# The queries of chunks 1 to 3 as three fp32r products of high and low parts

## The chip, the cores and the metric

The kernel runs on one core of one Trainium2 chip. The metric is the device time of one execution in microseconds. The core has five engines that run side by side and meet only in semaphores: TensorE (PE, with its weight loads PEld), VectorE (DVE), ScalarE (ACT), GpSimd (POOL), and SyncE (SP), which issues most transfers. Matrix products land in PSUM, which has eight banks of 128 partitions x 512 fp32 numbers.

## The reference, cut to what matters

Three blocks one behind the other, each on a layer norm of its input and added to it: cross attention of 64 items (32 queries of 256 channels, 257 context rows of 192 channels, 16 heads), an attention over the items, and a mixture of eight experts. The change touches one line of the first block, the projection of the queries.

```python
q = (query @ Wq + bq).reshape(B, Nq, H, D).transpose(0, 2, 1, 3)   # B 64, Nq 32, Cq 256, H 16, D 16
k = (key_value @ Wk + bk) ...                                        # Nkv 257, Ckv 192
v = (key_value @ Wv + bv) ...
attn = jnp.einsum('bhqd,bhkd->bhqk', q, k) * scale                   # then clip and softmax
x = jnp.einsum('bhqk,bhkd->bqhd', attn, v).reshape(B, Nq, Cq)
return x @ Wo + bo
```

## The kernel before

The cross attention runs over 64 tiles, i = 0 to 63, one item each. It is a software pipeline: in iteration i TensorE (loop at line 1127) does `scores(i)`, `weigh(i-2)`, the two `transp(i-1)`, then `kproj(i+1)` in two halves and `vproj(i+1)`. DVE (loop at 882) does `clip(i,0)`, `negmax(i,0)`, `clip(i,1)`, `ptevac(i-1)`, `negmax(i,1)`, then `total`, `recip` and `otevac` of older tiles. ACT (loop at 969) does the other `ptevac`, the four exponentials, and the copies of keys and values out of PSUM. POOL (loop at 761) splits the context into high and low parts, spreads the queries for the heads (`spread`), and does the small products `tailpart` and `norm`.

The queries are made for 512 rows at a time, a chunk of 16 tiles: chunk 0 before the loop, chunks 1 to 3 in iterations 11/12, 27/28 and 43/44. In iteration 16c-5 TensorE transposes the normalised input (`qturn`, 1015, two banks "t") and ACT copies both banks to `xnT` (`qchunk`, 912), which gives `s_t0e`. In iteration 16c-4, behind `vproj`, TensorE makes the products with the fp32 weights `Wq` (`qproj`, 1024, two banks "q"), and DVE adds the bias and scales at the end of its own iteration (`qevac`, 812).

Keys and values are already made of fp32r products: each operand is copied to fp32r (the high part), the difference to the fp32 original is the low part, and high x high, high x low and low x high are summed in PSUM (`terms`, 1033). Weights of the later stages are split in the same way in quiet iterations: ACT makes the high part (994), POOL the low part (`wlow`, 691).

PSUM banks 4 to 7 go round in a fixed order, the list `uses` (226 to 239). Each entry is a key, and the semaphore with its value that tells that the bank's content has been read. `take` (1008) gives the n-th use bank 4 + n % 4 and first waits until use n-4 is released. In iteration 11 the list has p(10,0), p(10,1), k(12,0), k(12,1), v(12), t(1,0), t(1,1), and in iteration 12 p(11,0), p(11,1), k(13,0), k(13,1), v(13), q(1,0), q(1,1). Every engine works through its own instructions in order, and the order above is written out by hand.

Of the kernel before, what the change touches and what calls it, by code (L numbers as in the profile page):

```python
# [6 lines left out]
ALU = mybir.AluOpType  # L7
# [24 lines left out]
C_MN = 168  # L32
# [43 lines left out]
def build(nc, d, out, vx_d, w1_d, y_d, g_d):  # L76
    ctx = ExitStack()
    with ctx:
# [56 lines left out]
        s_c = sem("s_c")  # L135
        s_w = sem("s_w")
        s_w3 = sem("s_w3")
        s_c2 = sem("s_c2")
        s_id = sem("s_id")
        s_v2 = sem("s_v2")  # L140
        s_fill = sem("s_fill")
# [74 lines left out]
        Mb = put("Mb", [128, 2, 4, 16])  # L216
        rc = put("rc", [128, 2, 4])
        nm = put("nm", [128, 2, 4])
        wst.append(put("wst1", [128, 1024]))
        whl.append(put("whl1", [128, 2, 1024], F32R))  # L220

# [5 lines left out]
        for i in range(-1, T + 1):  # L227
            if 1 <= i:
                uses += [(("p", i - 1, p), s_pte[p], i) for p in range(2)]
            if i + 1 < T:  # L230
                uses += [(("k", i + 1, p), s_ke, 2 * (i + 1) + p + 1) for p in range(2)]
            if i + 1 < T:
                uses += [(("v", i + 1), s_ve, i + 2)]
            if i == 0:
                uses += [(("b",), s_basee, 1)]
            if 0 <= i < 48 and i % 16 == 11:
                uses += [(("t", i // 16 + 1, k), s_t0e, 2 * (i // 16 + 1) + k + 1) for k in range(2)]
            if 0 <= i < 48 and i % 16 == 12:
                uses += [(("q", i // 16 + 1, m), s_qe, 2 * (i // 16 + 1) + m + 1) for m in range(2)]
        spot = {u[0]: n for n, u in enumerate(uses)}  # L240
# [3 lines left out]

        def whalves(n):

            if n == 0:
                return [WaR[:, w, :, :].rearrange("p k n -> p (k n)") for w in range(2)]
            return [WcR[:, w, n - 1, :] for w in range(2)]
# [312 lines left out]
        with nc.Block() as block:  # L562

            @block.sync
            def _(sp):
# [26 lines left out]
                load_ctx(1)  # L592
                sp.dma_start(Wo[:, :, :], d["xWo"].rearrange("(k p) n -> p k n", p=128)).then_inc(s_w3, 16)
                sp.dma_start(bcc[:, :, :], bcast(d["brow"], 128)).then_inc(s_w3, 16)
                sp.dma_start(cst[:, C_MN:C_END], d["cst"][:, C_MN:C_END]).then_inc(s_c2, 16)
                load_ctx(2)
                sp.wait_ge(s_vxe, 2)
                sp.wait_ge(s_v1, 2)
# [37 lines left out]
                for j in range(3, NPAIR):  # L636
                    load_ctx(j)
                    for q in range(2 * E):
                        if j == 6 + 3 * q // 2:
                            for h in range(2):  # L640
                                pace(j, h)
                                load_piece(q, h)
                    for q in range(2 * E):
                        if j == 8 + 3 * q // 2:
                            for n in range(4):
                                pace(j, 2 + n)
                                store_split(q, n // 2, n % 2)
                    if j in (5, 12, 20):
                        c = (5, 12, 20).index(j) + 1
                        load_tails(16 * c, 16, s_vt[c])  # L650
                    if j in (7, 15):
                        load_x((7, 15).index(j) + 2)
                    if j == 3:

                        sp.wait_ge(s_wl, 1)
                        sp.dma_start(wA[:, 0, :].rearrange("p (k n) -> p k n", k=2),
                                     d["aW"].rearrange("(k p) n -> p k n", p=128)).then_inc(s_w2, 16)
                        sp.dma_start(wA[:, 1, :], d["cwT"][0:128].rearrange("p k n -> p (k n)")).then_inc(s_w2, 16)
                        sp.dma_start(WgT[:, :, :], d["WgT"].rearrange("(k p) n -> p k n", p=128)).then_inc(s_w2, 16)
                    if j == 10:  # L660
                        sp.wait_ge(s_wsd, 4)
                        sp.dma_start(wA[:, 0, :], d["cwT"][128:256].rearrange("p k n -> p (k n)")).then_inc(s_ws, 16)
                    if j == 25:

                        sp.wait_ge(s_t0, 8)
                        for n in range(8):
                            pace(j, 2 + n)
                            t0 = 4 * (n // 2)
                            sp.dma_start(xb[64 * (n % 2):64 * (n % 2) + 64, t0:t0 + 4, :], xbd[n % 2][:, t0:t0 + 4, :]
                                         ).then_inc(s_xb, 16)  # L670

            @block.gpsimd
            def _(g):
# [16 lines left out]

                def wlow(n, h):

                    g.wait_ge(s_wsh, n + 1)
                    hi, lo = whalves(n)
                    c = slice(256 * h, 256 * h + 256)
                    g.tensor_tensor(lo[:, c], wA[:, n % 2, c], hi[:, c].bitcast(F32), ALU.subtract).then_inc(s_wsd, 1)
                    g.wait_ge(s_wsd, 2 * n + h + 1)

                rstd(0)

# [60 lines left out]
                for i in range(T + 2):  # L761
                    if i + 1 < T:
                        spread(i + 1)
                    if 1 <= i <= T:
                        tailpart(i - 1)

                    j, n = (i + 3) // 2 if i % 2 else (i + 2) // 2, 0 if i % 2 else 2
                    go = 2 <= j < NPAIR
                    if go:
                        split(j, n)  # L770
                    if i >= 2:
                        norm(i - 2)
                    if go:
                        if n == 2:
                            g.wait_ge(s_m, i - 1)
                        split(j, n + 1)

                    q = (i - 9) // 3
                    if i % 3 == 0 and 0 <= q < 2 * E:
                        g.wait_ge(w_h, q + 1)  # L780
                        g.tensor_tensor(whl[q % 2][:, 1, :], wst[q % 2][:, :], whl[q % 2][:, 0, :].bitcast(F32),
                                        ALU.subtract).then_inc(w_l, 1)

                    if i % 16 == 6 and i < 48:
                        rstd(i // 16 + 1)
                    if i in (10, 12, 14, 16, 30, 32):
                        m = (10, 12, 14, 16, 30, 32).index(i)
                        wlow(m // 2, m % 2)
                    if i == 49:
                        g.wait_ge(s_xb, 128)  # L790
                        g.wait_ge(s_basee, 1)
                    if 49 <= i < 49 + NTILE:
                        m = i - 49
                        g.tensor_tensor(xb[:, m, :], xb[:, m, :], base[:, :], ALU.add).then_inc(s_xbb, 1)
                        g.wait_ge(s_xbb, m + 1)

            @block.vector
            def _(v):
# [37 lines left out]

                def base_row():

                    v.wait_ge(s_c2, 16)
                    v.wait_ge(s_base, 1)  # L840
                    v.tensor_tensor(base[:, :], held("b")[:, 0:C], bcc[:, 0, :], ALU.add).then_inc(s_basee, 1)

                def clip(i, p):
                    v.wait_ge(s_s, 2 * i + p + 1)
# [37 lines left out]
                for i in range(T + 3):  # L882
                    if i < T:
                        clip(i, 0)
                        negmax(i, 0)
                        clip(i, 1)
                        if i >= 1:
                            ptevac(i - 1)
                        negmax(i, 1)
                    if 2 <= i < T + 2:  # L890
                        total(i - 2)
# [19 lines left out]
            def _(a):  # L911
                def qchunk(c):
                    for k in range(2):
                        a.wait_ge(s_t0, 2 * c + k + 1)
                        if c:
                            a.wait_ge(s_q, 2 * c)
                        a.activation(xnT[:, k, :], held("t", c, k)[:, :], ACT.Copy).then_inc(s_t0e, 1)

                def highs(j):
                    a.wait_ge(s_cx[j], 48)  # L920
# [48 lines left out]
                for i in range(-1, T + 1):  # L969
# [16 lines left out]
                    if i % 3 == 2 and 0 <= q < 2 * E:  # L986
                        a.wait_ge(w_d[q % 2], 32 * (q // 2 + 1))
                        if q >= 2:
                            a.wait_ge(w_s[q % 2], 64 * (q // 2))
                        a.activation(whl[q % 2][:, 0, :], wst[q % 2][:, :], ACT.Copy).then_inc(w_h, 1)  # L990
                    if i in (9, 11, 29):
                        n = (9, 11, 29).index(i)
                        a.wait_ge([s_w2, s_w2, s_ws][n], [48, 48, 16][n])
# [3 lines left out]
            def _(t):  # L997
# [25 lines left out]

                def qproj(c):
                    t.wait_ge(s_t0e, 2 * c + 2)
                    for m in range(2):
                        b = take("q", c, m)
                        for k in range(2):
                            mm = t.matmul(b[:, :], Wq[:, k, 128 * m:128 * m + 128], xnT[:, k, :],
                                          start=(k == 0), stop=(k == 1))  # L1030
                        mm.then_inc(s_q, 1)

                def terms(b, bi):
# [81 lines left out]

                def base_row():

                    t.wait_ge(s_c2, 16)
                    t.wait_ge(s_w3, 16 * 2)
                    b = take("b")  # L1120
                    for k in range(2):
                        mm = t.matmul(b[:, 0:C], bcol[:, 4 + k:5 + k].broadcast_to([128, 128]), Wo[:, k, :],
# [87 lines left out]
            def _(t):  # L1210
                t.wait_ge(s_ote, T)
                t.wait_ge(s_w2, 48)
                t.wait_ge(s_wsd, 6)

                def take(*key):
                    n = place[key]
# [807 lines left out]
```

## Time and profile before

| | |
|---|---|
| median of 3 runs | 610.33 us (609.41 to 612.26) |
| the profiled execution | 609.9 us, span 608.1 us |
| TensorE busy | 588.9 us, 97% |
| DVE busy | 457.2 us, 75% |
| ACT busy | 337.2 us, 55% |
| POOL busy | 321.3 us, 53% |
| mean granted TensorE clock | 0.994 |

The profile is of one execution; times in it count from the span's start. An engine's busy time is the union of its instructions. A row of the timeline is "start, length, engine, line, operation, output <- inputs", with the idle time before it and who ended it in square brackets. Matmuls are pipelined: their rows overlap, so the distance from start to start is what one costs. The attention loop runs from about 15 to 334 us.

### The profile page before, as it was taken

Reading aid. Unit: us, or ns where it says so; the run is one execution under the profiler, and the core shown is the slowest. Engines: PE = TensorE matmul, PEld = TensorE weight load, DVE = VectorE, ACT = ScalarE, POOL = GpSimd, SP = SyncE. Lnnn points to the kernel's source line nnn. Section 1 sums busy time; section 2 is a strip of 40 time slices with the busy share of each in tenths; the row PEclk is TensorE's granted clock in tenths of the full one; section 3 lists DMA queues with packets and bytes.
Section 4 is the critical chain, followed back from the end, with each engine's and each line's share of the span. In section 5 each row is a group of like instructions: output and inputs, shape, how many; then the busy total and the mean of one; then the engine's idle time right before and its main releaser. Section 6 shows DMA issues by size and latency. Waiting matters only on the chain.

```text
span 608.1 us, 21788 instructions
## 1 busy us (share of the span) xinstructions
PE 588.9 (97%) x8367; PEld 482.3 (79%) x8367; DVE 457.2 (75%) x1069; ACT 337.2 (55%) x751; POOL 321.3 (53%) x474
## 2 busy tenths in 40 slices
PE   9999999999999999999999999998899999998977
PEld 4888878888788887888887788884588888884865
DVE  4688877888678886777777676888788888883654
ACT  3677868878687786777776156454323333330211
POOL 3457858787578777678874311111433333314771
PEclk9999999999999999999999999998999999999899
DMA  8724653776354855875400797257333334434884
GB/s 226 182 74 110 172 180 99 246 183 212 110 193 127 246 157 175 199 230 153 150 16 3 307 416 285 67 178 253 128 131 130 131 130 133 131 124 131 232 251 118
DMA packets 66069, 102.11 MB, mean 168 GB/s; under 512 B 15504, under 2 KB 42192, under 8 KB 65072
## 3 DMA queue, kind: packets, MB, share of 16 engines
q1 hardware_dynamic: 60672, 86.42, 44.2%
q0 software_dynamic: 4432, 13.50, 8.1%
q8 instruction: 69, 1.13, 0.8%
q10 hardware_dynamic: 864, 0.79, 0.5%
q14 instruction: 32, 0.26, 0.1%
HBM read 69.42 MB, written 31.26 MB: 166 GB/s over the span
## 4 chain that ended last, share of the span: by engine, by line
PE 54%; POOL 23%; issue 14%; DVE 3%; DMA 2%; ACT 2%; POOLq 0%; DVEq 0%; ACTq 0%
PE bank L1936 12%; PE scores L1936 6%; PE bank L1044 5%; PE bank L1051 5%; PE bank L1076 4%; POOL hA L718 4%; POOL lA L714 4%; POOL cg L1768 4%; POOL hA L710 4%; PE scores L1092 3%; PE scores L1065 3%; POOL Mb L751 2%; POOL tm L742 2%; PE bank L1961 1%; PE scores L1921 1%
## 5 line engine op out<-in xcount | busy, mean ns | idle before, releaser
L850 DVE TENSOR_SCALAR Pm<-scores 128x514 f32<-128x514 f32 x128 | 88.0, 688 | 52.8 <-PE scores L1065 52.6
L966 ACT ACTIVATE Pm<-Pm,nm 128x257 f32<-128x257 f32 x256 | 115.8, 505 | 2.5 <-DVE nm L855 2.5
L855 DVE TENSOR_REDUCE nm<-Pm 128x2 f32<-128x514 f32 x128 | 87.4, 683 | 2.2
L1757 POOL DMA_INDIRECT Xg<-y_d,inv x39 | 37.0, 950 | 82.9 <-PE scores L1921 70.1
L961 ACT ACTIVATE PT<-bank 128x512 f32<-128x512 f32 x64 | 38.3, 598 | 74.0 <-PE bank L1076 74.0
L1044 PE MATMUL bank<-hA,wH 128*128 128x258 f32 x256 | 75.2, 304 | 0.3 <-POOL hA L718 0.3
L1076 PE MATMUL bank<-cst,Pm 128*128 128x128 f32 x512 | 70.0, 279 | 0.0
L1044 PE MATMUL bank<-hA,wL 128*128 128x258 f32 x256 | 69.3, 281 | 0.0
L1051 PE MATMUL bank<-wH,hA 128*128 128x256 f32 x256 | 69.0, 281 | 0.0
L1051 PE MATMUL bank<-wL,hA 128*128 128x256 f32 x256 | 68.9, 280 | 0.0
L1895 ACT ACTIVATE sg<-sg 128x512 f32<-128x512 f32 x39 | 24.7, 632 | 77.6 <-DVE sg L1782 77.6
L1936 PE MATMUL bank<-W,xh 128*128 x208 | 66.7, 402 | 0.5 <-DVE xl L1849 0.5
L1092 PEld LDWEIGHTS scores<-Vs,PT 128*32 128x32 f32 x4096 | 41.2, 110 | 25.2 <-issue 24.1
L751 POOL TENSOR_TENSOR Mb<-Os,rc 128x64 f32<-128x64 f32 x64 | 21.6, 338 | 73.6 <-DVE rc L875 73.2
L1076 PEld LDWEIGHTS bank<-cst,Pm 128*128 128x128 f32 x512 | 54.9, 141 | 2.9 <-issue 0.8
L944 ACT ACTIVATE kT<-bank,bcol 128x258 f32<-128x258 f32 x128 | 53.5, 469 | 2.6 <-PE bank L1044 2.3
L1044 PEld LDWEIGHTS bank<-hA,wH 128*128 128x128 f32 x256 | 48.4, 189 | 1.2 <-issue 1.1
L1044 PEld LDWEIGHTS bank<-hA,wL 128*128 128x128 f32 x256 | 48.5, 189 | 0.2 <-issue 0.2
L1051 PEld LDWEIGHTS bank<-wL,hA 128*128 128x128 f32 x256 | 48.2, 188 | 0.0
L1051 PEld LDWEIGHTS bank<-wH,hA 128*128 128x128 f32 x256 | 48.2, 188 | 0.0
L1092 PE MATMUL scores<-Vs,PT 128*32 128x17 f32 x4096 | 47.5, 186 | 0.2 <-issue 0.2
L1768 POOL DMA_INDIRECT cg<-g_d,pi x32 | 31.7, 992 | 26.5 <-DMA g_d<-gg 17.0
(280 smaller groups left out, 1434.1 us busy)
## 6 DMA issues: line engine op xcount, KB each, us to landing
w_d<-whl SPq DMA_DIRECT2D x64, 256.0 KB, 3.5
W<-w_d SPq DMA_DIRECT2D x6, 2048.0 KB, 16.7
g_d<-gg SPq DMA_DIRECT2D x39, 256.0 KB, 2.4
wst<-in_W1T SPq DMA_DIRECT2D x32, 256.0 KB, 3.3
cx<-in_ctxT SPq DMA_DIRECT2D x31, 258.0 KB, 3.0
cx<-in_ctxT SPq DMA_DIRECT2D x62, 129.0 KB, 3.5
bb<-in_b SPq DMA_DIRECT2D x8, 512.0 KB, 6.3
W<-w_d SPq DMA_DIRECT2D x5, 512.0 KB, 5.3
```

Source lines behind the costliest of these rows:

```text
L850: v.tensor_scalar(Pm[:, i % 2, 2 * p:2 * p + 2, :], S4[:, 2 * p:2 * p + 2, 0:NK], -CLAMP, CLAMP, ALU.max, ALU.min).then_inc(s_cl, 1)
L855: v.tensor_reduce(nm[:, i % 2, 2 * p:2 * p + 2], Pm[:, i % 2, 2 * p:2 * p + 2, :], AX.X, ALU.max, negate=True).then_inc(s_nm, 1)
L944: a.activation(kT[:, i % 2, m, :], held("k", i, m)[:, 0:NKP], ACT.Identity, bias=bcol[:, 2 + m:3 + m]).then_inc(s_ke, 1)
L961: a.activation(PT[:, i % 2, 0, :, :].rearrange("p a b -> p (a b)"), held("p", i, 0)[:, :], ACT.Copy).then_inc(s_pte[0], 1)
L966: a.activation(Pm[:, i % 2, g, :], Pm[:, i % 2, g, :], ACT.Exp, bias=nm[:, i % 2, g:g + 1]).then_inc(s_ex, 1)
L1044: mm = t.matmul(b[:, 0:NKP], w[:, 128 * m:128 * m + 128], c, start=(e == 0), stop=(e == 4))
L1051: mm = t.matmul(b[:, C * c:C * c + C], x[:, 128 * c:128 * c + 128], w[:, C:2 * C], start=(e == 0), stop=(e == 4))
L1076: mm = t.transpose(b[:, o:o + 128], Pm[:, i % 2, 2 * p + gg, 128 * c:128 * c + 128], ident)
L1092: mm = t.matmul(pO[r, VH * g:VH * g + VH], PT[:, i % 2, p, 2 * gg + c, r], Vs[:, i % 4, c, 4 * (h // 2) + g, h % 2, :], start=first, stop= ...
L1757: g.indirect_dma_start(out=Xg[:, i % 3, :], out_offset=None, in_=y_d, in_offset=bass.IndirectOffsetOnAxis(ap=inv[:, i:i + 1], axis=0)).the ...
L1768: g.indirect_dma_start(out=cg[:, j % 8, k, :], out_offset=None, in_=g_d, in_offset=bass.IndirectOffsetOnAxis(ap=pi[:, k, j:j + 1], axis=0) ...
L1936: mm = t.matmul(o, x[:, i % 2, k, :], W1[:, bass.DynSlice(w + (part * 2048 + k * 1024 + 512 * h), 512)], start=(k == 0 and part == 0 and x ...
```

## The change

Chunk 0 stays as it is. For chunks 1 to 3 ACT copies the transposed input to fp32r (`xqR[:, 0]`), DVE subtracts that from the bank for the low part (`xqR[:, 1]`, the new function `query_lows`, placed in iteration 16c-4 between `ptevac` and the second `negmax`), and `qproj` sums three fp32r products for each half of the channels where it had plain fp32 ones. The release of the "t" banks in `uses` becomes `s_xl`, given by `query_lows`. `Wq` is split too: the high part by ACT at i=4, the low part by POOL at i=5 and i=7. The counts of `s_wsh` and `s_wsd` shift by one and two for that. The semaphore `s_c2` is merged into `s_w3`. Two new arrays, `WqR` (4 KB of a partition) and `xqR` (8 KB), are put ahead of `wst1` and `whl1`.

```diff
@@ -135,7 +135,7 @@
         s_c = sem("s_c")
         s_w = sem("s_w")
         s_w3 = sem("s_w3")
-        s_c2 = sem("s_c2")
+        s_xl = sem("s_xl")
         s_id = sem("s_id")
         s_v2 = sem("s_v2")
         s_fill = sem("s_fill")
@@ -216,6 +216,8 @@
         Mb = put("Mb", [128, 2, 4, 16])
         rc = put("rc", [128, 2, 4])
         nm = put("nm", [128, 2, 4])
+        WqR = put("WqR", [128, 2, 2, C], F32R)
+        xqR = put("xqR", [128, 2, 2, 512], F32R)
         wst.append(put("wst1", [128, 1024]))
         whl.append(put("whl1", [128, 2, 1024], F32R))
 
@@ -234,7 +236,7 @@
             if i == 0:
                 uses += [(("b",), s_basee, 1)]
             if 0 <= i < 48 and i % 16 == 11:
-                uses += [(("t", i // 16 + 1, k), s_t0e, 2 * (i // 16 + 1) + k + 1) for k in range(2)]
+                uses += [(("t", i // 16 + 1, k), s_xl, 2 * (i // 16) + k + 1) for k in range(2)]
             if 0 <= i < 48 and i % 16 == 12:
                 uses += [(("q", i // 16 + 1, m), s_qe, 2 * (i // 16 + 1) + m + 1) for m in range(2)]
         spot = {u[0]: n for n, u in enumerate(uses)}
@@ -244,6 +246,8 @@
 
         def whalves(n):
 
+            if n == -1:
+                return [WqR[:, w, :, :].rearrange("p k n -> p (k n)") for w in range(2)]
             if n == 0:
                 return [WaR[:, w, :, :].rearrange("p k n -> p (k n)") for w in range(2)]
             return [WcR[:, w, n - 1, :] for w in range(2)]
@@ -592,7 +596,7 @@
                 load_ctx(1)
                 sp.dma_start(Wo[:, :, :], d["xWo"].rearrange("(k p) n -> p k n", p=128)).then_inc(s_w3, 16)
                 sp.dma_start(bcc[:, :, :], bcast(d["brow"], 128)).then_inc(s_w3, 16)
-                sp.dma_start(cst[:, C_MN:C_END], d["cst"][:, C_MN:C_END]).then_inc(s_c2, 16)
+                sp.dma_start(cst[:, C_MN:C_END], d["cst"][:, C_MN:C_END]).then_inc(s_w3, 16)
                 load_ctx(2)
                 sp.wait_ge(s_vxe, 2)
                 sp.wait_ge(s_v1, 2)
@@ -658,7 +662,7 @@
                         sp.dma_start(wA[:, 1, :], d["cwT"][0:128].rearrange("p k n -> p (k n)")).then_inc(s_w2, 16)
                         sp.dma_start(WgT[:, :, :], d["WgT"].rearrange("(k p) n -> p k n", p=128)).then_inc(s_w2, 16)
                     if j == 10:
-                        sp.wait_ge(s_wsd, 4)
+                        sp.wait_ge(s_wsd, 6)
                         sp.dma_start(wA[:, 0, :], d["cwT"][128:256].rearrange("p k n -> p (k n)")).then_inc(s_ws, 16)
                     if j == 25:
 
@@ -690,11 +694,12 @@
 
                 def wlow(n, h):
 
-                    g.wait_ge(s_wsh, n + 1)
+                    g.wait_ge(s_wsh, n + 2)
                     hi, lo = whalves(n)
                     c = slice(256 * h, 256 * h + 256)
-                    g.tensor_tensor(lo[:, c], wA[:, n % 2, c], hi[:, c].bitcast(F32), ALU.subtract).then_inc(s_wsd, 1)
-                    g.wait_ge(s_wsd, 2 * n + h + 1)
+                    whole = Wq[:, :, :].rearrange("p k n -> p (k n)") if n < 0 else wA[:, n % 2, :]
+                    g.tensor_tensor(lo[:, c], whole[:, c], hi[:, c].bitcast(F32), ALU.subtract).then_inc(s_wsd, 1)
+                    g.wait_ge(s_wsd, 2 * n + h + 3)
 
                 rstd(0)
 
@@ -783,9 +788,9 @@
 
                     if i % 16 == 6 and i < 48:
                         rstd(i // 16 + 1)
-                    if i in (10, 12, 14, 16, 30, 32):
-                        m = (10, 12, 14, 16, 30, 32).index(i)
-                        wlow(m // 2, m % 2)
+                    if i in (5, 7, 10, 12, 14, 16, 30, 32):
+                        m = (5, 7, 10, 12, 14, 16, 30, 32).index(i)
+                        wlow(m // 2 - 1, m % 2)
                     if i == 49:
                         g.wait_ge(s_xb, 128)
                         g.wait_ge(s_basee, 1)
@@ -836,9 +841,18 @@
 
                 def base_row():
 
-                    v.wait_ge(s_c2, 16)
+                    v.wait_ge(s_w3, 48)
                     v.wait_ge(s_base, 1)
                     v.tensor_tensor(base[:, :], held("b")[:, 0:C], bcc[:, 0, :], ALU.add).then_inc(s_basee, 1)
+
+                def query_lows(c):
+
+                    for k in range(2):
+                        v.wait_ge(s_t0e, 2 * c + k + 1)
+                        if c >= 2:
+                            v.wait_ge(s_q, 2 * c)
+                        v.tensor_tensor(xqR[:, 1, k, :], held("t", c, k)[:, :], xqR[:, 0, k, :].bitcast(F32), ALU.subtract
+                                        ).then_inc(s_xl, 1)
 
                 def clip(i, p):
                     v.wait_ge(s_s, 2 * i + p + 1)
@@ -886,6 +900,8 @@
                         clip(i, 1)
                         if i >= 1:
                             ptevac(i - 1)
+                        if i < 49 and i % 16 == 12:
+                            query_lows(i // 16 + 1)
                         negmax(i, 1)
                     if 2 <= i < T + 2:
                         total(i - 2)
@@ -912,9 +928,10 @@
                 def qchunk(c):
                     for k in range(2):
                         a.wait_ge(s_t0, 2 * c + k + 1)
-                        if c:
+                        if c >= 2:
                             a.wait_ge(s_q, 2 * c)
-                        a.activation(xnT[:, k, :], held("t", c, k)[:, :], ACT.Copy).then_inc(s_t0e, 1)
+                        a.activation(xqR[:, 0, k, :] if c else xnT[:, k, :], held("t", c, k)[:, :], ACT.Copy
+                                     ).then_inc(s_t0e, 1)
 
                 def highs(j):
                     a.wait_ge(s_cx[j], 48)
@@ -988,6 +1005,8 @@
                         if q >= 2:
                             a.wait_ge(w_s[q % 2], 64 * (q // 2))
                         a.activation(whl[q % 2][:, 0, :], wst[q % 2][:, :], ACT.Copy).then_inc(w_h, 1)
+                    if i == 4:
+                        a.activation(whalves(-1)[0], Wq[:, :, :].rearrange("p k n -> p (k n)"), ACT.Copy).then_inc(s_wsh, 1)
                     if i in (9, 11, 29):
                         n = (9, 11, 29).index(i)
                         a.wait_ge([s_w2, s_w2, s_ws][n], [48, 48, 16][n])
@@ -1023,11 +1042,21 @@
 
                 def qproj(c):
                     t.wait_ge(s_t0e, 2 * c + 2)
+                    if c:
+                        t.wait_ge(s_xl, 2 * c)
+                        t.wait_ge(s_wsd, 2)
                     for m in range(2):
                         b = take("q", c, m)
-                        for k in range(2):
-                            mm = t.matmul(b[:, :], Wq[:, k, 128 * m:128 * m + 128], xnT[:, k, :],
-                                          start=(k == 0), stop=(k == 1))
+                        s = slice(128 * m, 128 * m + 128)
+                        if c == 0:
+                            for k in range(2):
+                                mm = t.matmul(b[:, :], Wq[:, k, s], xnT[:, k, :], start=(k == 0), stop=(k == 1))
+                        else:
+                            e = 0
+                            for k in range(2):
+                                for w, x in ((0, 0), (1, 0), (0, 1)):
+                                    mm = t.matmul(b[:, :], WqR[:, w, k, s], xqR[:, x, k, :], start=(e == 0), stop=(e == 5))
+                                    e += 1
                         mm.then_inc(s_q, 1)
 
                 def terms(b, bi):
@@ -1115,8 +1144,7 @@
 
                 def base_row():
 
-                    t.wait_ge(s_c2, 16)
-                    t.wait_ge(s_w3, 16 * 2)
+                    t.wait_ge(s_w3, 48)
                     b = take("b")
                     for k in range(2):
                         mm = t.matmul(b[:, 0:C], bcol[:, 4 + k:5 + k].broadcast_to([128, 128]), Wo[:, k, :],
@@ -1210,7 +1238,7 @@
             def _(t):
                 t.wait_ge(s_ote, T)
                 t.wait_ge(s_w2, 48)
-                t.wait_ge(s_wsd, 6)
+                t.wait_ge(s_wsd, 8)
 
                 def take(*key):
                     n = place[key]
```

## Rows read from the trace of the kernel before

**Rows 1.** The page, part 1: busy us, share of span, instructions.

```profile
PE 588.9 (97%) x8367; PEld 482.3 (79%) x8367; DVE 457.2 (75%) x1069; ACT 337.2 (55%) x751; POOL 321.3 (53%) x474
```

**Rows 2.** Windows: busy us of each engine in a stretch, clock, DMA share, GB/s.

```profile
102.00:150.00 48.00, 48.00 (x1156) 42.43 (x1149) 40.66 (x94) 38.01 (x85) 38.99 (x57) 1.00 0.68 200
```

**Rows 3.** The chain of work, 69 to 90 us: start, us, what.

```profile
74.55 0.62 PE scores L1065 x16
...
76.86 1.21 PE bank L1044 x10
...
79.26 3.43 PE bank L1029 x8
82.69 0.62 PE scores L1065 x16
...
87.38 0.62 PE scores L1065 x16
```

**Rows 4.** Timeline of TensorE, scores and first key weights, tile 12's iteration.

```profile
74.47 0.69 PE L1065 MATMUL scores<-kT,QF 32*64 32x258 f32 x16
...
76.59 0.19 PEld L1044 LDWEIGHTS bank<-hA,wH 128*128 128x128 f32 x1
```

**Rows 5.** Timeline of DVE, tile 12's iteration.

```profile
77.14 0.68 DVE L862 COPY PT<-bank 128x512 f32<-128x512 f32 x1
77.74 0.68 DVE L855 TENSOR_REDUCE nm<-Pm 128x2 f32<-128x514 f32 x1
...
81.01 0.75 DVE L816 TENSOR_SCALAR qT<-bank,bcol 128x512 f32<-128x512 f32 x1 [2.06 <-PE bank L1029]
```

**Rows 6.** Timeline of ACT, the copies out of the "t" banks.

```profile
74.20 1.08 ACT L917 ACTIVATE xnT<-bank 128x512 f32<-128x512 f32 x2
```

**Rows 7.** Cover on ACT and POOL: groups, waits and timeline, 22 to 79 us.

```profile
L961 ACT ACTIVATE PT<-bank 128x512 f32<-128x512 f32 x4 | 2.4, 600 | 5.1 <-PE bank L1076 5.1
...
L696 POOL TENSOR_TENSOR WaR<-wA,WaR x2: 732/734/735, 71.0 to 82.9; 128x256 fp32r<-128x256 f32 x2
...
POOL Mb L751 <- DVE rc L875: 12.6, 8, 1.9
...
78.84 0.29 POOL L751 TENSOR_TENSOR Mb<-Os,rc 128x64 f32<-128x64 f32 x1 [2.97 <-DVE rc L875]
```

**Rows 8.** Timeline of TensorE and DVE, tile 44's iteration (chunk 3).

```profile
234.00 0.69 PE L1065 MATMUL scores<-kT,QF 32*64 32x258 f32 x16
...
237.26 0.68 DVE L855 TENSOR_REDUCE nm<-Pm 128x2 f32<-128x514 f32 x1
```

**Rows 9.** Like forms elsewhere: the chain at 437 us, DVE's low parts (ns).

```profile
437.30 2.77 PE bank L1936 x12
...
446.27 2.74 PE bank L1936 x12
...
L1444 DVE TENSOR_TENSOR xTl<-scores,xTh x5: 659/681/692, 353.7 to 388.3; 128x512 fp32r<-128x512 f32 x5
```

**Rows 10.** Timeline: hand-overs from DVE to a waiting TensorE.

```profile
433.46 0.42 DVE L1849 TENSOR_TENSOR xl<-scores,xh 128x256 fp32r<-128x256 f32 x1
434.04 0.31 PEld L1936 LDWEIGHTS bank<-W,xh 128*128 128x128 f32 x2 [0.76 <-issue]
...
561.97 0.75 DVE L1871 SCALAR_TENSOR_TENSOR zc<-cg,cmb,zc 128x512 f32<-128x512 f32 x1
562.77 0.29 PEld L1947 LDWEIGHTS scores<-cst,zc 128*128 128x128 f32 x2 [2.30 <-DVE zc L1871]
```

**Rows 11.** Two gaps of TensorE and the windows behind them (clock third from last).

```profile
562.77 1.12 PE L1947 MATMUL scores<-cst,zc 128*128 128x128 f32 x4 [2.06 <-DVE zc L1871]
...
562.90:566.00 3.10, 3.10 (x10) 2.65 (x11) 1.24 (x2) 0.60 (x1) 2.49 (x3) 0.50 0.72 202
...
592.97 0.66 PE L1947 MATMUL scores<-cst,zc 128*128 128x128 f32 x4 [1.71 <-DVE zc L1871]
...
593.00:596.30 3.30, 3.30 (x20) 2.97 (x21) 2.19 (x5) 1.07 (x2) 1.68 (x2) 1.00 0.81 210
```

## The prediction

> **What bounds the kernel now.** I read the page's first part first. TensorE is busy for 588.9 of 608.1 us (97%) [rows 1], so a microsecond put into its queue, or a microsecond for which it must wait, is likely to be a microsecond of the time. That is an average, so the stage that the change touches comes next: the windows of the attention loop [rows 2]. From 102 to 150 us TensorE is busy for all 48.00 us at clock 1.00, while DVE, ACT and POOL have 7 to 10 us of room each. The chain of work over one chunk border [rows 3] gives the beat: the scores of tiles 12, 13 and 14 stand in it at 74.55, 82.69 and 87.38. An ordinary tile takes 82.69 to 87.38 = 4.69 us; tile 12 takes 8.14, with the 3.43 us of qproj in it. In this stretch the chain names TensorE alone. So the loop runs at TensorE's pace, and what the change does has to be read as: how many microseconds fewer in qproj, and does TensorE begin to wait for somebody.
>
> **The change, part by part.**
>
> *qproj of chunks 1 to 3.* Removed: four fp32 products of 512 columns, which the trace shows as 8 records that take 3.43 us of the chain [rows 3]. Added: twelve fp32r products of 512 columns with 128x128 weights. The same set is in the trace: an expert step of line 1936 is twelve such products and takes 2.74 to 2.77 us of the chain [rows 9], say 2.75 or 0.229 each. That is 0.68 us less per chunk. The Trainium skill (TensorE: Matmul & The Clock Gate, section "Back-to-back issue gap") gives about 131 ns for one 512-column product in a sustained stream of loads and products. By that figure the twelve would be 1.57 us and the saving 1.86 per chunk, an estimate from the page; this trace's 0.229 for the same pair of instructions speaks against it.
>
> *The bank of the transposed queries.* This is where I expect the cost. The four PSUM banks go round in the order of `uses`. After the two "t" banks of chunk c come p(11,0), p(11,1), then k(13,0), k(13,1): so kproj of tile 13, first half, waits in `take` for the release of ("t", c, 0), and the second half for ("t", c, 1). Before, the release was s_t0e, given by ACT's two copies from 74.20 to 75.28 [rows 6], over a microsecond before TensorE asked at 76.59 [rows 4]. Now the release is s_xl, which DVE gives after query_lows, and DVE runs query_lows in iteration 12 behind clip(12,0), negmax, clip(12,1) and the copy of p(11,1). In the trace DVE starts that copy at 77.14 and its next instruction at 77.74 [rows 5]. In the new order that next instruction is the low part of k=0. Its form (128x512 fp32r from PSUM and SBUF) is in the trace on line 1444: 0.68 us [rows 9]. So the bank is free at 77.74 + 0.68 = 78.42. The hand-over from DVE to TensorE's weight load is 0.05 us in one row (DVE ends at 561.97 + 0.75 = 562.72, load at 562.77) and 0.16 in another (433.46 + 0.42 = 433.88, load at 434.04) [rows 10]. The first weight load of kproj then starts at 78.47 to 78.58 in place of 76.59: a wait of 1.88 to 1.99 us, new, on the engine that bounds. I take 1.90, as most of DVE's path to it is plain and the 0.16 row has a register read beside it. Queued behind this wait are kproj, vproj, qproj and the scores of tile 13; all of it moves back as one.
>
> The second low part ends 0.60 later (DVE's starts lie 0.60 apart [rows 5]), at 79.02. The first half of kproj takes 1.20 / 2 = 0.60 us [rows 3], so the second half asks at about 79.1: no second wait. qproj itself waits for s_xl as well, long past then. The other chunks look alike: in the third the scores start at 234.00 and DVE's slot for the low part is at 237.26 [rows 8], 3.26 us later, as 77.74 is 3.27 after 74.47, the start of the scores of tile 12 [rows 4]; the second has the same pattern. So three times the same.
>
> *Work that only moves DVE, ACT and POOL.* DVE gets 2 x 0.60 = 1.20 us in iteration 12, ahead of negmax(12,1). That makes exp of heads 2 and 3 of tile 12 later. They now wait for negmax to end at about 79.6 and for the two kevac copies behind the delayed kproj, so they run from about 80.4 to 81.3. The transposes that need them come after the scores of tile 13, at 83.9 or later: covered by over 2 us. DVE waited 2.06 us for qproj [rows 5], which takes up its 1.20. The query evacuation keeps its place right behind the last product, so clip(13,0) follows it as before. The copy of the high part on ACT has the size of the copy that it replaces. One more ACT copy of 512 columns at i=4 costs 0.60 us (the copy of 128x512 in [rows 7]) against an idle 5.1 / 4 = 1.28 us before each transposed-P copy; two more POOL subtractions of 0.73 at i=5 and i=7 go against a POOL that waits 12.6 / 8 = 1.6 us for recip in an iteration there [rows 7]. All at nothing. If their cover were gone, they would cost 0.60 and 1.46 us once. DVE's s_xl waits stand behind ACT's copies that ended long before. POOL's norm(10), which waits for recip, comes 1.2 us later; POOL had waited 2.97 us there [rows 7], and its next product for TensorE, the query spread of tile 14, is due 4.7 us after tile 13's scores: covered. The merged semaphores (s_c2 into s_w3) wait for the same three transfers. SP's own order is unchanged; its paced transfers go with the tiles.
>
> *The sum.* Per chunk +1.90 - 0.68 = +1.22 us, three chunks +3.7 us (bounds 3 x 1.20 to 3 x 1.31: 3.6 to 3.9). The profiled execution took 609.9 us (span 608.1), 0.4 under the median of the runs. 609.9 + 3.7 = 613.6, and on the median 610.33 + 3.7 = 614.0. Everything behind the loop starts from its last tile, so I let the shift through one for one.
>
> **The rivals.**
>
> *A. TensorE's clock falls after the new gap.* A gap of some 1.9 us in front of a dense stream is new in this loop. The combine stage at the end has two such gaps: after 2.06 us idle the clock is 0.50 (1.2 GHz of 2.4) for at least 3.1 us, after 1.71 us idle it stays at 1.00 [rows 11]. The new gap lies between them. The loop before it is dense, which speaks against a fall; its length speaks for one. A fall costs about half of 3.1 us or a little more, 1.6 us, since TensorE bounds: one fall gives 615.6, three give 618.8. The Trainium skill (TensorE: Matmul & The Clock Gate, "What's actually happening") puts it as "the default state is throttled, and activity releases the throttle"; by that rule thin activity should throttle it again, and the fall after 2.06 us agrees.
>
> *B. The wait does not bite: no slower, a little faster.* If DVE gave the "t" banks back before TensorE asks for them, at 76.59, only the saving stays: 3 x 0.68 = 2.0 us, 608.3 us. The point is a wait of 0.68 us per chunk: below it the change wins. For it: DVE has some 7 us of room in 48 [rows 2], so it is not short of time as such. Against it: its idle time in these iterations lies before the scores and before qproj's end, and the code puts the low parts behind three instructions that start only with them; DVE's slot would have to come 1.2 us sooner.
>
> *C. Part of the loss is given back.* TensorE's pause lets POOL, ACT and the transfers get ahead, and where TensorE waits a little for them later, that wait goes. With TensorE busy for all of a 48 us stretch [rows 2] there is little to win: 0.3 to 1 us, 613.0 to 613.7, or down to 611.8 if the low part is handed over more quickly than its row.
>
> *D. The change does not do what it says*: the products run as more than twelve passes, or at fp32's rate (12 x 0.86 = 10.3 us in place of 3.43, +20 us in all). The fp32r rows of the same size say no.
>
> **How the numbers follow.** Forecast, wait of 1.9 and clock kept: 0.50, own range 613.2 to 615.2. A: 0.26, 615.6 to 618.8. C: 0.15, 611.8 to 613.7. B: 0.08, 608 to 610.5. D: 0.01. The predicted time is 614.0. The range for 8 in 10 leaves out B and the cases with two or three falls: 611.3 to 617.5. Half a per cent, 3.05 us, is about what a measurement of this kernel can tell from no change, so "slower" begins at 613.4, close under my forecast. Slower: 0.42 from the forecast, 0.25 from A and 0.02 from C and D, 0.69. Same: the rest of the forecast, nearly all of C and half of B, 0.26. Faster: 0.05.
>
> **What would show it.** In the profile after: 24 fp32 records at line 1029's successor are gone and 36 fp32r ones stand there, about 2.75 us per chunk; TensorE idle for about 1.9 us before the first kproj product of tiles 13, 29 and 45, released by DVE's xqR; tile 12, 28 and 44 take about 9.4 us from scores to scores in place of 8.14; DVE's wait for qproj shrinks to under 2 us. All other tiles keep 4.69. The clock at the three places shows A. If the kproj products start at once, the bank argument is wrong; if the gap is there and the total is not, the loss came back behind the loop and one-for-one is wrong.

## The result

The changed kernel takes 615.64 us (median of 8 runs, 612.74 to 617.10) against 610.95 us of the kernel before (8 runs, 608.21 to 612.26): ratio 1.0077 with a 95% interval of 1.0051 to 1.0102. It is slower by 3.1 to 6.2 us. 614.0 was forecast.

The page of the changed kernel, part 1 and, from part 5, the group of key products that now waits (against [rows 1]). The columns of a group are: line, engine, operation, output<-inputs, shape, count, busy us, mean ns, idle before and who ended it.

```profile
span 614.6 us, 21828 instructions
...
PE 589.0 (96%) x8379; PEld 482.8 (79%) x8379; DVE 460.8 (75%) x1075; ACT 338.8 (55%) x752; POOL 323.6 (53%) x476
...
L1073 PE MATMUL bank<-hA,wH 128*128 128x258 f32 x256 | 75.3, 305 | 5.1 <-DVE xqR L854 4.9
```

TensorE is not busier (589.0 us against 588.9), the span is longer, and 4.9 us of idle time in front of kproj, absent before, end with DVE's low part (line 854). The 2 us that the cheaper products save hardly show in the busy time: in the loop it is 312.1 us in place of 313.0, behind the loop 264.5 in place of 263.4. The chain over the first chunk border (start, length, what), to be read against [rows 3]:

```profile
74.55 0.64 PE scores L1094 x16
...
76.54 0.68 DVE Pm L864
77.22 0.10 DVE PT L876
77.32 0.42 issue
77.74 0.69 DVE xqR L854
78.43 0.04 issue
78.48 1.46 PE bank L1073 x10
79.93 1.18 PE bank L1080 x10
81.11 2.76 PE bank L1058 x12
83.87 0.62 PE scores L1094 x16
...
88.56 0.62 PE scores L1094 x16
```

From scores to scores the step over the border is 83.87 - 74.55 = 9.32 us, against 8.14 before. qproj takes 2.76 in place of 3.43. But the chain now leaves TensorE: from the scores it runs through DVE's clip, copy and low part, and comes back to kproj only at 78.48. Only 1.62 us of the wait are idle time of TensorE's products; the rest is a first key piece of 1.46 in place of 1.21 [rows 3]. The next step is the ordinary 4.69 again. DVE, ACT and TensorE in the same stretch, from the timeline (against [rows 4 to 6]):

```profile
75.21 0.69 DVE L864 TENSOR_SCALAR Pm<-scores 128x514 f32<-128x514 f32 x1 [2.02 <-PE scores L1094]
77.74 1.28 DVE L854 TENSOR_TENSOR xqR<-bank,xqR 128x512 fp32r<-128x512 f32 x2
82.54 0.75 DVE L821 TENSOR_SCALAR qT<-bank,bcol 128x512 f32<-128x512 f32 x1 [2.40 <-PE bank L1058]
...
74.20 1.08 ACT L933 ACTIVATE xqR<-bank 128x512 fp32r<-128x512 f32 x2
80.34 0.90 ACT L983 ACTIVATE Pm<-Pm,nm 128x257 f32<-128x257 f32 x2
...
78.47 0.19 PEld L1073 LDWEIGHTS bank<-hA,wH 128*128 128x128 f32 x1 [1.86 <-DVE xqR L854]
```

ACT has emptied both "t" banks by 75.28. DVE is idle for 2.02 us up to 75.21. It reads the same banks only at 77.74. TensorE's first weight load of kproj starts at 78.47, where it started at 76.59 before.

Read over the whole loop, by the start of each tile's scores (a step is named by the tile it leads into): the steps into tiles 13, 29 and 45 were 8.15, 8.13 and 8.15 us and are 9.32, 9.32 and 9.34, together 3.55 us more. The last tile's scores start 5.87 us later (333.81 against 327.94). The other 2.3 us are what is left of three longer steps of this execution, 2.8 us together, and some slightly shorter ones: 5.12 into tile 20 (4.69 before), 6.31 into tile 28 (5.57) and 6.29 into tile 55 (4.69). From the last tile's scores to the end it takes 280.8 us in place of 280.1. In the step into tile 55, TensorE stops in the middle of vproj and no engine is named as the releaser:

```profile
295.11 0.38 PE L1080 MATMUL bank<-wH,lA 128*128 128x256 f32 x1 [1.34 <-issue]
```

Whether such steps belong to the change was an open question, and one run below is for it.

### The profile page after: what moved, and what is told of

It is laid out like the page before. It is cut to its first block, busy times and chain, and to the rows that moved or that the text cites. A ratio compares the mean times of both kernels' runs of the same rounds, so it can differ in the third digit from the quotient of the medians.

```text
span 614.6 us, 21828 instructions
## 1 busy us (share of the span) xinstructions
PE 589.0 (96%) x8379; PEld 482.8 (79%) x8379; DVE 460.8 (75%) x1075; ACT 338.8 (55%) x752; POOL 323.6 (53%) x476
## 4 chain that ended last, share of the span: by engine, by line
PE 51%; POOL 22%; issue 15%; DVE 8%; DMA 2%; ACT 1%; POOLq 0%; DVEq 0%; ACTq 0%
PE bank L1964 12%; PE scores L1964 6%; PE bank L1073 6%; PE bank L1080 5%; PE bank L1105 4%; POOL cg L1796 4%; POOL hA L723 4%; POOL lA L719 4%; POOL hA L715 3%; PE scores L1121 3%; PE scores L1094 3%; POOL Mb L756 2%; POOL tm L747 2%; PE scores L1949 1%; PE bank L1989 1%
```

## The experiments

The first four ran on one chip beside the kernel before at 610.82 us (29 runs). The last four ran on another, where the kernel before takes 628.91 us (7 runs). The kernel before was timed there, but no trace of it is kept from that chip. The changed kernel's loop has ordinary steps of the same length on both; the time behind it is longer (298.6 us from the last tile's scores to the end in run 5, against 280.8). Ratios are always to the kernel before on the same chip.

**1. The low parts moved into DVE's idle time.**

```diff
                     if i < T:
+                        if i < 49 and i % 16 == 12:
+                            query_lows(i // 16 + 1)
                         clip(i, 0)
...
                             ptevac(i - 1)
-                        if i < 49 and i % 16 == 12:
-                            query_lows(i // 16 + 1)
                         negmax(i, 1)
```

> The changed kernel with one move: DVE makes the two low parts at the head of iteration 12 (28, 44), ahead of clip(i,0), in the time in which it waited 2.02 us for the scores, and no longer behind ptevac. Theory (the new cost is only the wait for the t banks): the banks come back at about 76.1, before TensorE asks at 76.59, no gap; scores to scores over the three borders 7.5 us in place of 9.32 (and 8.15 before the change); in all 3 x 0.68 = 2.0 us under the kernel before, about 608.5 to 609, 5.5 us under the changed kernel. Rival (the DVE work itself or the delayed clip costs): borders stay above 8.15, no gain on before. Rival (something behind the loop costs): borders 7.5 but the total no better than before.

Measured: 608.94 us (12 runs), ratio 0.9975 (0.9954 to 0.9996). All three steps over the borders are 7.45 us. Its chain over the first border:

```profile
75.25 0.62 PE scores L1094 x16
75.87 0.67 PE scores L1121 x51
76.54 1.02 PE bank L1105 x8
77.56 1.18 PE bank L1073 x10
78.75 1.18 PE bank L1080 x10
79.93 2.77 PE bank L1058 x12
82.70 0.62 PE scores L1094 x16
```

TensorE alone is in it, from scores to scores 7.45 us. In the timeline of DVE and ACT one sees what the move costs and that it is covered:

```profile
75.53 1.29 DVE L854 TENSOR_TENSOR xqR<-bank,xqR 128x512 fp32r<-128x512 f32 x2 [1.62 <-ACT xqR L933]
76.74 0.68 DVE L864 TENSOR_SCALAR Pm<-scores 128x514 f32<-128x514 f32 x1
...
78.18 0.91 ACT L983 ACTIVATE Pm<-Pm,nm 128x257 f32<-128x257 f32 x2 [0.24 <-DVE nm L869]
```

clip starts 0.8 us later behind the scores than in the changed kernel (76.74 - 75.18 against 75.21 - 74.48, the scores starting in the timeline at 75.18 and 74.48), ACT waits 0.24 us for the maxima, and nothing of it comes to TensorE. The DVE work is the same, only its place differs, so the loss was in the place. This version beats both kernels: 3 x (8.14 - 7.45) = 2.1 us in the steps, 0.2 to 2.8 us in the times.

**2. The same DVE work, but the banks released by ACT.**

```diff
-                uses += [(("t", i // 16 + 1, k), s_xl, 2 * (i // 16) + k + 1) for k in range(2)]
+                uses += [(("t", i // 16 + 1, k), s_t0e, 2 * (i // 16 + 1) + k + 1) for k in range(2)]
...
-                        v.tensor_tensor(xqR[:, 1, k, :], held("t", c, k)[:, :], xqR[:, 0, k, :].bitcast(F32), ALU.subtract
+                        v.tensor_tensor(xqR[:, 1, k, :], xqR[:, 0, k, :].bitcast(F32), xqR[:, 0, k, :].bitcast(F32), ALU.subtract
```

> The changed kernel with DVE's low-part instructions in their place and of the same size, but reading the high part from SBUF and not the t bank, which ACT's copy releases as before the change. Left out: the low part of the queries comes out as zero, so two of the six terms with it add nothing. Theory: same DVE, ACT, POOL and TensorE work, no wait at kproj, borders 8.15 - 0.68 = 7.47 us, total 2.0 us under before. Rival (DVE's 1.2 us in the middle of the iteration delays TensorE by itself, through exp and transposes): borders above 8.15.

Measured: 609.91 us (10 runs), ratio 0.9974 (0.9951 to 0.9998). The steps are 7.58, 8.11 and 7.57 us. kproj no longer waits at any border, with DVE's low parts still behind its copy of P. So the wait is that for the bank, and the delay of DVE's second maximum by 1.2 us is not what costs. The steps are above 7.47 because now qproj reaches the low parts early. In the second border it waits for them outright, since DVE's two subtractions took 1.81 us there and 1.28 at the others:

```profile
157.84 1.81 DVE L854 TENSOR_TENSOR xqR<-xqR 128x512 fp32r<-128x512 f32 x2
...
159.74 3.00 PE L1058 MATMUL bank<-xqR,WqR 128*128 128x512 f32 x12 [0.43 <-issue]
```

DVE ends at 159.65, qproj starts at 159.74. In the changed kernel this second wait is hidden behind the first.

**3. The wait with the old products.**

```diff
-                        if c == 0:
+                        if True:
                             for k in range(2):
-                                mm = t.matmul(b[:, :], Wq[:, k, s], xnT[:, k, :], start=(k == 0), stop=(k == 1))
+                                x = xqR[:, 0, k, :].bitcast(F32) if c else xnT[:, k, :]
+                                mm = t.matmul(b[:, :], Wq[:, k, s], x, start=(k == 0), stop=(k == 1))
```

> The changed kernel with its low parts and bank waits, but with the four fp32 products of before in qproj of chunks 1 to 3, reading the high part. Left out: the low part of the queries is computed and not used. Theory: the wait costs 1.86 us per border and the products take 3.43 again: borders 8.15 + 1.86 = 10.0 us, three times, total 5.6 us over before (about 616.5). Rival (part of the saving in the changed kernel came from elsewhere): borders other than 9.32 + 0.68 = 10.0.

Measured: 616.87 us (4 runs), ratio 1.0108 (1.0077 to 1.0140). The steps are 10.00, 10.01 and 10.01 us, 1.86 to 1.88 above the kernel before. Its chain:

```profile
77.81 0.69 DVE xqR L854
78.50 0.04 issue
78.54 1.47 PE bank L1074 x10
80.01 1.18 PE bank L1081 x10
81.19 3.43 PE bank L1054 x8
84.62 0.62 PE scores L1095 x16
```

The two terms are independent: the wait is 1.87 by itself, the products give back 0.68, and 8.14 + 1.87 - 0.68 = 9.33 is what the changed kernel shows.

**4. The splitting of the weights alone.** To the kernel before are added the copy on ACT and the two subtractions on POOL, with their counts:

```diff
+                    if i == 4:
+                        a.activation(whalves(-1)[0], Wq[:, :, :].rearrange("p k n -> p (k n)"), ACT.Copy).then_inc(s_wsh, 1)
...
-                    if i in (10, 12, 14, 16, 30, 32):
-                        m = (10, 12, 14, 16, 30, 32).index(i)
-                        wlow(m // 2, m % 2)
+                    if i in (5, 7, 10, 12, 14, 16, 30, 32):
+                        m = (5, 7, 10, 12, 14, 16, 30, 32).index(i)
+                        wlow(m // 2 - 1, m % 2)
```

> The kernel before with only the splitting of the query weights added: one ACT copy at i=4, two POOL subtractions at i=5 and i=7, results not used. Theory: hidden, tiles 4 to 9 keep 4.67 to 4.70 us, total as before within the noise. Rival (ACT or POOL work late somewhere, or the extra code shifts things): some tile between 4 and 9 longer by 0.3 us or more; or single longer tiles far from the change, as tiles 20, 28 and 55 of the changed kernel had (+0.43, +0.73, +1.6).

Measured: 609.67 us (10 runs), ratio 0.9990 (0.9963 to 1.0017). Each step into tiles 4 to 12 lies within 0.15 us of its length before, the steps over the borders are 8.14, 8.14 and 8.13. Hidden, as costed. The only step that is over 0.3 us longer than before, 5.31 into tile 3 (4.73), comes ahead of the added work; run 5 returns to it.

**5. The changed kernel once more**, unaltered, for the three long steps.

> The changed kernel unaltered, once more. The profiled execution of it was 6.5 us longer in span than the one of before, of which the three borders are 3.54 us; tiles 20, 28 and 55 were longer by 0.43, 0.73 and 1.6 us with no engine named as releaser. Theory (these three are chance, of the kind that both kernels have in single executions): borders 9.32 to 9.34 again, the long tiles elsewhere or absent, span near 611.6 plus or minus 1.5; median 3.5 to 4.5 us over before. Rival (the change brings them, as by the moved code or transfers): tile 55 is long by over 1 us again and the loop is about 5.9 us longer than before.

Measured: 632.17 us (5 runs), ratio 1.0049 (1.0030 to 1.0068), 3.1 us with 1.9 to 4.3 as its bounds. The steps over the borders are 9.34, 9.34 and 9.33 us. The steps into tiles 20 and 55 are ordinary here (4.78 and 4.69), that into 28 is 5.55 as before the change. So the three long steps do not come in every execution of the changed kernel. But this execution has a longer one, 8.56 us into tile 3 (4.73 before). TensorE stops there shortly before the end of `weigh`, again with no engine named, and its clock is 0.50 behind the stop:

```profile
30.18 0.29 PE L1121 MATMUL scores<-Vs,PT 128*32 128x17 f32 x2 [2.25 <-issue]
...
30.40:32.40 2.00, 2.00 (x12) 2.00 (x11) 0.69 (x1) 0.85 (x2) 0.00 (x0) 0.50 0.07 21
```

With it the last tile's scores start at 335.84, 7.9 us later than before the change, of which the borders are 3.6 and this step 3.8.

Such stops are not spread at random: they come back in front of the same product, with another length each time. The one into tile 3 stands in the traces of runs 1, 2, 4, 5, 6 and 7 (0.39 to 2.25 us), the one in vproj on the way into tile 55 in that of the result and in runs 1, 6, 7 and 8 (0.24 to 1.34 us). The first is in run 4 without the new products or the new wait. The second is in none of the traces of the kernel before and of runs 2 to 5, so from one trace or two of a kernel it can't be told whether the change makes it more likely. Others have their own places (6.06 into tile 52 in the next run). What makes them was not found.

**6. The low parts one instruction earlier**, ahead of the copy of P and behind the second clip.

```diff
+                        if i < 49 and i % 16 == 12:
+                            query_lows(i // 16 + 1)
                         if i >= 1:
                             ptevac(i - 1)
-                        if i < 49 and i % 16 == 12:
-                            query_lows(i // 16 + 1)
                         negmax(i, 1)
```

> The changed kernel with the low parts one instruction earlier: ahead of ptevac(i-1), behind clip(i,1). DVE's slots lie 0.60 us apart. Theory: the gap before kproj is 1.86 - 0.60 = 1.26 us, borders 9.32 - 0.60 = 8.72 us, total about 1.8 us under the changed kernel. Rival: the banks of the transposed P are copied 1.2 us later and something that needs them waits; then borders above 8.72.

Measured (one execution): steps of 8.70, 8.71 and 8.71 us, 0.62 under the changed kernel.

```profile
79.60 0.39 PE L1073 MATMUL bank<-hA,wH 128*128 128x258 f32 x1 [1.02 <-DVE xqR L854]
```

DVE's place sets the wait, one for one. The single time, 633.32 us, says nothing against it: it is one run, and its steps into tiles 3, 52 and 55 are 6.39, 6.06 and 5.60 us long.

**7. and 8. One and two more additions ahead of the low parts**, to see what a longer gap does. In 8 the count is 2.

```diff
                 def query_lows(c):
+                    for z in range(1):
+                        v.tensor_tensor(xnT[:, z, :], Wq[:, :, :].rearrange('p k n -> p (k n)'), Wq[:, :, :].rearrange('p k n -> p (k n)'), ALU.add)
```

> The changed kernel with one more DVE addition of 128x512 fp32 (from SBUF to a free tile) ahead of the low parts. Theory: the gap grows by that instruction, 0.6 to 0.9 us, to 2.5 to 2.8, and the borders to 9.9 to 10.2 us, as long as TensorE's clock stays. Rival A (the clock falls behind such a gap): clock 0.50 for about 3 us behind at least one border and that border longer by a further 1.6 us, to about 11.6.

> The same with two more additions. Theory without a fall of the clock: gap 3.1 to 3.7 us, borders 10.5 to 11.1. Rival A: as before the change the clock fell after 2.06 us of idleness, it should fall here at most borders: clock 0.50 in the windows behind them and borders of 12.1 to 12.7 us.

Measured (one execution each): steps of 11.45, 11.67 and 11.46 us with one, 12.06, 13.59 and 11.76 us with two; times 639.87 and 641.66 us. One addition moves DVE by 0.60 us (1.10 at the second border of each run, see the last section), so without anything else the steps of 7 should be 9.93, 10.43 and 9.93 us and those of 8 10.53, 11.03 and 10.53. They are longer than that by 1.5, 1.2 and 1.5 us in 7 and by 1.5, 2.6 and 1.2 us in 8. The 12.1 to 12.7 expected of 8 with a fall of the clock fit the first border alone: the second is longer, the third shorter. TensorE's gap and the windows around it in 7 (the clock is the third number from the end):

```profile
80.29 0.39 PE L1075 MATMUL bank<-hA,wH 128*128 128x258 f32 x1 [2.22 <-DVE xqR L856]
...
76.00:80.20 4.20, 2.07 (x88) 1.50 (x72) 3.75 (x7) 3.24 (x7) 1.07 (x1) 1.00 0.57 215
...
81.00:84.00 3.00, 3.00 (x16) 3.00 (x15) 0.92 (x4) 1.75 (x4) 1.99 (x3) 0.50 0.02 5
...
85.00:88.00 3.00, 3.00 (x54) 1.98 (x56) 1.50 (x3) 0.10 (x1) 2.92 (x5) 1.00 0.51 156
```

Behind the gap the same products run at 0.50, 1.2 GHz. In the chain of 7 kproj and vproj take 2.04 and 2.13 us where they take 1.46 and 1.18 in the changed kernel:

```profile
80.29 2.04 PE bank L1075 x10
82.33 2.13 PE bank L1082 x10
84.46 2.75 PE bank L1060 x12
```

This is rival A, one dose later than in the change. The same window behind the gap of the changed kernel, from run 5:

```profile
82.35 0.39 PE L1073 MATMUL bank<-hA,wH 128*128 128x258 f32 x1 [1.62 <-DVE xqR L854]
...
82.40:86.00 3.60, 3.60 (x26) 3.38 (x27) 1.58 (x5) 2.26 (x5) 1.93 (x3) 1.00 0.02 5
```

With the gap of 1.62 us (1.86 for the weight loads) the clock stayed at 1.00 at all nine borders of the three traces that have it, with 2.22, 2.71 and 2.22 us it fell at all three of run 7, with 2.82, 3.32 and 2.82 us at all three of run 8. At the second border of run 8 it stayed at 0.50 from 163 to 169 us, which is the 2.6 us. The unnamed stops fit in: behind 1.34 us (the changed kernel, tile 55) and 1.47 us (run 6, tile 3) the clock stayed at 1.00, behind 2.25 us (run 5) it was 0.50.

## Why the prediction was right, and where it was off

*Which wait.* It is the one named: kproj's first half on the bank of ("t", c, 0), released by DVE, three times in the kernel and nowhere else. Runs 1 and 2 show it from two sides, once by moving the work and once by moving the release.

*Its size.* The low part was put at 77.74 and the weight load at 78.47 to 78.58; they came at 77.74 and 78.47, the lower bound, that of the zc row in [rows 10]. The wait is 1.86 to 1.88 us in place of 1.90. So the hand-over is that of the zc row, 0.05 us; what makes the other row 0.16 was not tested.

*The products.* 2.75 was taken from the expert steps [rows 9], 2.76 measured. The figure from the Trainium skill (TensorE: Matmul & The Clock Gate, section "Back-to-back issue gap"), which would have made qproj 1.57 us, an estimate from the page, does not hold here.

*No second wait.* The second half of kproj follows the first at once in the timeline, and qproj waits for nothing in the changed kernel. Run 2 shows that this is narrow for qproj: without the gap ahead of it, it waits for DVE's low parts, 0.1 us by the steps at two borders and 0.43 at the third.

*Hidden work.* Run 4 for the weights. exp of heads 2 and 3 was put at about 80.4 and ran at 80.34. POOL's wait for recip was to grow from 2.97 by 1.2, and is 4.18:

```profile
80.04 0.29 POOL L756 TENSOR_TENSOR Mb<-Os,rc 128x64 f32<-128x64 f32 x1 [4.18 <-DVE rc L889]
```

*A miss.* DVE's wait for qproj was to shrink under 2 us. It grew from 2.06 to 2.40. I counted the 1.20 us that DVE gets and forgot that qproj itself moves back by the gap: 2.06 + 1.88 - 1.20 - 0.33, the last for a first half of six products that is 1.38 us long in place of 1.71. Nothing depends on it, as the sum did not use it.

*The sum.* +1.22 per chunk was forecast, +1.18 is measured in both traces of the changed kernel, 3.55 in all against 3.7. The medians say 4.7 (3.1 to 6.2) on one chip and 3.1 (1.9 to 4.3) on the other. Both intervals hold 3.55. The 615.64 lies above the 613.2 to 615.2 given for the likeliest case. That it is the 615.6 given for one fall of the clock is chance: in both traces of the changed kernel the clock is 1.00 behind all three gaps. The part above 3.55, about 1 us, is not explained. Two things of that size vary in the traces: the unnamed stops of run 5's section, and the time from the last tile's scores to the end, 278.8 to 280.8 us in the traces of the two kernels and of runs 1 to 4. Whether the change has a share in either stays open.

*The rivals.* B, the wait that does not bite, is what run 1 makes of the change; its price, -2.0 us, came out as 2.1 in the steps. The idle time lay where the prediction said, ahead of the scores, and I held it against the rival without asking whether ACT's copies are ready by then. They are: they end at 75.28. A did not happen at 1.86 us and its price was right: 1.2 to 1.5 us per fall (once 2.6) against 1.6. It was one DVE instruction away. The sentence of the Trainium skill (TensorE: Matmul & The Clock Gate, "What's actually happening") quoted there fits runs 7 and 8: the throttle came back after idleness and was released again under load. C gave nothing back: the steps into tiles 14 to 19 are 4.67 to 4.70, before they were 4.67 to 4.72.

## What to carry to other kernels

A semaphore that says "this buffer is read" is a cost on whoever takes the buffer next, so when a second reader is added to a PSUM bank, look up the next use of that bank in the rotation and compare its due time with the slot of the new reader in its own engine's order, not with that engine's load: here an engine with 7 us of room in 48 made the busiest engine wait 1.87 us, three times. Fewer passes on the bottleneck (0.68 us per chunk) are worth making only with the new reader ahead of the other work, in the idle time before its inputs arrive. And a gap on TensorE has a second price that begins suddenly: one more instruction of 0.6 us in front of the release cost 2.1 us.

## What the runs showed of the hardware

In this loop gaps of 1.62 us in front of kproj left TensorE's clock at 1.00 nine times in nine, and gaps of 2.22 to 3.32 us brought it to 0.50 six times in six. Lengths in between were not tried.

TensorE stopped for up to 2.25 us with no engine named as the releaser. Two such stops came back in front of the same product, in six and in five of the ten traces; the cause is open.

An addition or subtraction of 128x512 on DVE with both inputs in SBUF takes 0.68 us, and 1.18 to 1.21 us at the second border of runs 2, 7 and 8. Each time it began while POOL was at its low part of the context (line 719 or its like), and at the other borders POOL was idle. The form that reads a PSUM bank, in the changed kernel, began at 159.46 beside the same POOL work (158.57 to 159.85) and took 0.68, and so did the one of run 5 at 162.49 (POOL 161.83 to 163.11). Of run 2:

```profile
157.18 1.31 POOL L719 TENSOR_TENSOR lA<-cx,hA 128x516 fp32r<-128x516 f32 x1
...
L854 DVE TENSOR_TENSOR xqR<-xqR x6: 677/680/1206, 79.0 to 238.3; 128x512 fp32r<-128x512 f32 x6
```

In run 2 POOL ends at 157.18 + 1.31 = 158.49 and the first of DVE's two, begun at 157.84, lasts 1.21 us, so it ends 0.56 us after POOL. In run 7 POOL ends at 162.18 and DVE's at 161.56 + 1.18 = 162.74, again 0.56 us later: it looks like waiting until POOL is done, not like going slower. The Trainium skill (SBUF — State Buffer, section "Who interferes with whom") says that a DVE instruction with two SBUF inputs contends with a GpSimd instruction that reads SBUF, since its second input comes through the read interface that both share; the traces agree, as the form with only one input in SBUF was not held up. It was not tested by itself.
